# Graph-network kernel: a table lookup by one-hot matmuls on four quarter tiles of the array instead of two halves

## What is computed

```python
for l in range(3):
    f1 = relu(x[row] @ nb_W[l] + nb_b[l])
    f2 = relu(x[col] @ self_W[l] + self_b[l])
    h = relu(concatenate([f1, f2], axis=1) @ att1_W[l] + att1_b[l])
    log_alpha = (h @ att2_W[l] + att2_b[l])[:, 0]
    mask = clip(sigmoid(log_alpha) * (ZETA - GAMMA) + GAMMA, 0.0, 1.0)
    rowsum = segment_sum(mask, row, num_segments=n) + 1e-06
    d_inv_sqrt = clip(rowsum ** (-0.5), 0.0, 10.0)
    vals = mask * d_inv_sqrt[row] * d_inv_sqrt[col]
    x = segment_sum(vals[:, None] * x[col], row, num_segments=n)
    out = out + x
```

## Time and profile before

| what | us |
|---|---|
| median of 3 runs (11231.23 to 11239.19) | 11238.58 |
| span of the profiled execution, first to last instruction | 10215.4 |
| median less span (what lies around the span) | 1023.2 |
| TensorE busy in the span (matmuls) | 8439.0 |
| VectorE busy | 8039.4 |
| GpSimd busy | 4364.3 |
| ScalarE busy | 3166.6 |

### The profile page before, as it was taken

How to read it: one execution, slowest core, us unless ns; L and a number is a source line. 1 busy time by engine, 2 the same in 40 slices (tenths; PEclk the granted TensorE clock), 3 DMA queues, 4 the chain that set the end, 5 groups by cost and what they waited for, 6 DMA issues and landing times. The chain is left out here.

```text
span 10215.4 us, 720231 instructions
## 1 busy us (share of the span) xinstructions
PE 8439.0 (83%) x288671; PEld 7571.9 (74%) x288671; DVE 8039.4 (79%) x13908; ACT 3166.6 (31%) x6110; POOL 4364.3 (43%) x4880
## 2 busy tenths in 40 slices
PE   0113288888887999899997999899997999879996
PEld 0112177877776888799997888799997888768885
DVE  9998488888887777777777777777777777777775
ACT  0110156666663333300002333300001333333332
POOL 0002601111116888311114888521112888758883
PEclk9755599999998999999998999999998999989996
DMA  1001277777765555577775555467775555545552
GB/s 27 0 0 27 49 226 232 230 230 232 229 216 143 162 161 160 142 212 214 211 212 155 161 159 161 130 205 212 212 214 170 161 161 160 141 130 160 159 161 70
DMA packets 1005301, 1633.48 MB, mean 160 GB/s; under 512 B 260439, under 2 KB 743635, under 8 KB 1004831
## 3 DMA queue, kind: packets, MB, share of 16 engines
q1 hardware_dynamic: 954104, 1581.29, 52.8%
q0 software_dynamic: 51104, 50.97, 2.3%
HBM read 1345.54 MB, written 286.24 MB: 160 GB/s over the span
## 5 line engine op out<-in xcount | busy, mean ns | idle before, releaser
L1034 PE MATMUL bank<-tab,extra 128*64 128x64 bf16 x201684 | 3981.3, 197 | 389.0 <-DMA extra<-one_hots 230.4
L1034 PEld LDWEIGHTS bank<-tab,extra 128*64 128x64 fp8e4 x201684 | 3566.3, 112 | 877.4 <-issue 817.2
L739 POOL TENSOR_TENSOR planes<-planes 128x448 f32<-128x448 f32 (+1 forms) x2744 | 2610.2, 963 | 542.5 <-DVE planes L1767 476.1
L888 ACT CAST bank<-planes 128x448 f32<-128x448 bf16 (+1 forms) x2744 | 1515.1, 552 | 2289.5 <-DVE planes L1760 2283.0
L1142 PE MATMUL bank<-planes,extra 128*128 128x192 bf16 x19992 | 2098.2, 247 | 43.1 <-POOL planes L739 10.0
L669 POOL DMA_INDIRECT xg<-q_table,ixb x588 | 561.1, 954 | 3592.0 <-ACT ixb L837 3486.3
L1760 DVE TENSOR_TENSOR planes<-bank,mask_all 128x448 f32<-128x448 f32 (+2 forms) x2744 | 1699.0, 619 | 274.2 <-PE bank L1034 171.0
L1767 DVE TENSOR_TENSOR planes<-planes,bank 128x448 f32<-128x448 f32 (+1 forms) x2744 | 1727.4, 630 | 126.5 <-ACT bank L888 126.4
L1142 PEld LDWEIGHTS bank<-planes,extra 128*128 128x128 fp8e4 x19992 | 1584.2, 96 | 172.7 <-issue 55.0
L1640 DVE SCALAR_TENSOR_TENSOR extra<-bank,a2w 128x448 f32<-128x448 f32 (+1 forms) x2058 | 1300.2, 640 | 510.2 <-PE bank L1059 453.7
L1059 PE MATMUL bank<-plb,extra 128*128 128x64 bf16 x44982 | 1595.9, 194 | 14.4 <-ACT plb L869 9.0
(11 more groups left out here) (227 smaller groups left out, 4734.3 us busy)
## 6 DMA issues: line engine op xcount, KB each, us to landing
extra<-one_hots SPq DMA_DIRECT2D x1372, 368.0 KB, 3.3
extra<-one_hots SPq DMA_DIRECT2D x2156, 224.0 KB, 3.6
extra<-one_hots SPq DMA_DIRECT2D x588, 192.0 KB, 2.4
one_hots<-extra SPq DMA_DIRECT2D x490, 224.0 KB, 2.3
one_hots<-extra SPq DMA_DIRECT2D x294, 368.0 KB, 3.9
work<-slot_rows_cols SPq DMA_DIRECT2D x196, 368.0 KB, 5.2
work<-slot_rows_cols SPq DMA_DIRECT2D x294, 224.0 KB, 4.0
work<-slot_rows_cols SPq DMA_DIRECT2D x98, 192.0 KB
```

The lines of the kernel that those rows point to most:

```text
L739: nc.gpsimd.tensor_tensor(tiles(yrl[:, 2, a * C:b * C]), tiles(yrl[:, 1, a * C:b * C]), upper[:, 1, a:b, :], ALU.subtract).then_inc(low_re ...
L888: nc.scalar.copy(tiles(z_banks[g][:, 0:(b - a) * C]), upper[:, 0, a:b, :]).then_inc(high_ps, 1)
L1034: mm = pe.matmul(bank[half * S:(half + 1) * S, i * C:(i + 1) * C], oct_[:, k * P + half * S:k * P + (half + 1) * S], tab[:, at:at + C], st ...
```

## The change

In `cols`, a half tile of 64 slots is done as two quarters of 32 slots. The four quarters of a tile use four column quarters of the array and partitions 0, 32, 64 and 96 of the bank. The loops are turned round: the plane is outside, the quarters inside. Every matmul still moves 64 columns; there are 12 per tile instead of 6, each with a weight load of 32 columns instead of 64. Nothing else in the program differs.

```diff
+Q = 32
...
-                    for half in range(2):
-                        b = 2 * k + half
-                        for pl in range(NPL):
-                            at = (pl * NB + b) * C
-                            mm = pe.matmul(bank[half * S:(half + 1) * S, i * C:(i + 1) * C],
-                                           oct_[:, k * P + half * S:k * P + (half + 1) * S], tab[:, at:at + C],
+                    for pl in range(NPL):
+                        for q in range(4):
+                            at = (pl * NB + 2 * k + q // 2) * C
+                            mm = pe.matmul(bank[q * Q:(q + 1) * Q, i * C:(i + 1) * C],
+                                           oct_[:, k * P + q * Q:k * P + (q + 1) * Q], tab[:, at:at + C],
                                            start=(i == 0 and pl == 0), stop=True, skip_group_check=True)
```

## The result

The changed kernel takes 13,086.1 us (median of 4 runs, 13,084.0 to 13,095.0) beside 11,235.7 us for the kernel before on the same chip: ratio 1.165, 95% interval 1.163 to 1.167. It is slower by 16%; the forecast was 11,064 us and the range ended at 12,150. The profiled execution has a span of 13,083.9 us, 1.7 us less than its time as the runs are timed. So the 1,023 us that stood "around the span" ahead of the prediction did not exist; what they were, the experiments show.

What follows compares the result with a forecast made beforehand. TensorE was taken to bound six of seven loops. Lookups -225, first layer's edges -10 and code +60 gave -175 us, so 11,238.6 became 11,064 us; the range ran from 10,990 to 12,150.

Steps and rivals of the forecast that it cites:

- 1,023 us: Difference between the earlier kernel's profiled span and its median time, added unchanged to the predicted span of 10,040 us.
- Part (4): TensorE's code: more instructions mean more packets fetched in loops' first turns; nothing to 73 us, counted as +60.
- part (1): Lookups: a round falls from 31.9 to 29.3 ns as narrower weight loads hide; -225 us in six loops.
- rival D: Loops no longer fit where code is kept and are fetched each turn: +3,700 us, chance 0.04.
- What has to hold: Condition on the sequencer: hand over 24 instructions per tile in 88 ns, one per 3.7 ns.
- rival A: The sequencer becomes the bound in lookups; at 5.0 ns per instruction 12,000 us, chance 0.24.
- Part (3): VectorE, ScalarE, GpSimd and SyncE's loads keep their instructions and each wait stays in place; no cost counted.
- Rival B: Four streams in the array hinder each other, 36.9 ns per round: 11,730 us, chance 0.10.
- Part (2): Switches between full and split array, between lookups and scatters: number unchanged, cost put at nothing.
- TensorE bounds six loops: TensorE limits six of seven loops over the 98 blocks; small gains pass in full, losses at once.
- what would show it: Signs to look for in the profile: the long lookup run's length, block times, some 85 packets and none inside a loop.

Runs made afterwards that it cites:

- e5: The changed kernel run again, nothing else altered: 11,958.1 us beside 10,219.7 for the kernel before.
- e6: The changed kernel with 205 satisfied waits added at the start of TensorE's program: 11,134.3 us, 91 packets.
- f1: The changed kernel moved by 205 waits, with GpSimd's two indirect DMAs per block replaced by a clearing of the rows: 10,850.1 us; kernel before 11,252.7.
- f2: The kernel before, with GpSimd's two indirect DMAs per block replaced by a clearing of the rows: 10,323.3 us beside 11,252.7.
- e12: The same kernel as e6, timed in rounds on another chip: 12,361.3 us, ratio 1.090 to the kernel before.
- e8: The changed kernel with quarters only in every other tile of 128 slots, halves in the rest: 13,813.2 us.
- e2: The changed kernel with halves kept in the first layer's edges, quarters everywhere else: 12,760.2 us, 858 packets.
- e11: The changed kernel with 115 satisfied waits at the start of TensorE's program in place of 205: 15,991.4 us, 1,817 packets.
- f4: The kernel before, unchanged, profiled on a slower chip: 11,252.7 us.
- g2: The kernel before, with the second gather of each edge block waiting for group 1: 10,799.9 us beside 11,332.7, ratio 0.953.

## Why the prediction failed, step by step

The sum of -225 - 10 + 60 us failed at all its large terms. Part (4) counted code at 60 us, and one loop that is fetched again costs 824. Waits between groups and GpSimd's gathers stood at nothing; once TensorE uses instructions as fast as they come, they make most of the other 900. And part (1)'s -225 did not come.

On chips X the loss of 1,738 us (e5) splits into 824 us of code fetched again (e5 less e6), 527 us that stay without gathers (f1 less f2, on a chip Y), and the rest, 387 us, by the gathers. The 527 are carried over from one kind of chip to the other, so the last two are estimates. On chips Y e12 has 1,010 us without refetching, of which some 480 by the gathers. There the kernel before is torn in its edges, too, and the change adds almost nothing to later edges.

- **Part (4), code at +60 us, and rival D at 0.04.** The largest miss: 824 us for one loop fetched again on every second turn. Rival D named the mechanism, and its question was right ("no row here shows a loop of more than 4.5 packets"), but it was put aside by a figure for the whole memory. The loop of 6.8 packets is refetched or not by where its first instruction falls in a packet. D was right in kind for one of seven loops and wrong in size: it had every turn of all seven fetched, +3,700 us, at 3.0 us a packet. One turn of this loop takes 35 to 36 us and the next 19 to 22, with nine packets for the two, about 4 us apart.
- **What has to hold, and rival A.** The supply gives one instruction per 4.15 ns, slower than the 3.7 needed and quicker than the 5.0 at which the rival was priced. So this rival had the mechanism. By itself that is 24 x 4.15 = 100 ns per tile against 95.4: 0.2 us per block. What the rival missed is that the supply now has nothing in hand. The kernel before used an instruction per 7.95 ns, and 64 lay ready, 0.5 us of work. This stock covered every wait between groups, which costs 181 to 211 ns from start to start inside a run of f1 and does not show in f2, and on chips X it covered the gathers. With the 0.2 us the waits make 0.9 us per block of segment sums and 0.5 per block of later edges, some 450 us (f1 less f2); the first layer's edges lose nothing, and the rest of the 527 lies in the first turns of the loops and between them, where part (4) had put its 60.
- **Part (3), "GpSimd keeps its instructions", at nothing.** It keeps them, and their side effect, 387 us on chips X, had been covered by that stock. That the stock is what covered it is argued from its size (0.5 us) and the gaps' (0.23 to 0.34 us on chips X, up to 0.75 on chips Y, where halves are torn, too); no run changed the stock alone. No sum over TensorE's own rows could show it; the runs on chips Y did.
- **The 1,023 us between span and median.** They were taken as lying around the span. They were mostly the gathers' gaps on another chip: on one such chip 929 of 1,033 us go with them (f2). A gap of 10% between a profile and the runs that nothing explains was the one sign, ahead of the prediction, that TensorE could be starved.
- **Part (1), rounds of 29.3 ns.** Right while instructions lie ready: 29 ns for the rounds of four after the first, in the first 8 rounds of a run. The saving is gone by the end of the run: 84 quarters last as long as 42 halves. So the term of -225 us was worth nothing. Rival B, four streams in each other's way, is false: starts 3 to 4 ns apart and no longer round. This is what the Trainium skill's figure of some 4 ns per further tile (TensorE: Matmul & The Clock Gate, the section on packing small matmuls) says; the trace agrees.
- **Part (2), switches at nothing.** Their number did not change, and nothing shows a cost. A switch between the two widths is worth 125 ns (e8).
- **TensorE bounds six loops, a loss passes through at once.** Right.
- **Slips that change little.** The first edges' block has 843 matmuls, which makes 13.8 packets and +5 us, not 12.9 and +3. The second packet of the earlier trace rows lies 0.55 us into its window, not 0.8; the 6543.1 is right. Rival A at 5.3 ns with the code's 60 us would be 12,206; 12,150 belongs to about 5.2 ns.

Of what would show it: the run of 276 lasts 2.76 us (2.38 the 138 before), over rival A's mark of 2.7, and the packets rose to hundreds.

```profile
6005.44 2.76 PE L1034 MATMUL bank<-tab,extra 128*32 128x64 bf16 x276 [0.21 <-issue]
6008.40 0.86 PE L1059 MATMUL bank<-plb,extra 128*128 128x64 bf16 x24 [0.20 <-issue]
```

## What to carry to other kernels

Count instructions per microsecond, and not only busy time: an engine that uses them as fast as they come has no stock left, and every wait, hold-up or fetch that was hidden before is paid in full. A loop of TensorE that comes near 1,600 instructions should be kept shorter or looked at in its place in the program (the one of 1,616 was fetched again in e2 and e11, the one of 1,318 never); 205 idle instructions ahead of it were worth 7% here. If the same program is 10% slower in timed runs than in its profile, find out what the timed runs wait for before costing a change.

## What the runs showed of the hardware that was not expected

- A loop of 1,746 instructions of TensorE costs 9 us per turn more when it lies over eight packets of 16 KB, by count, than over seven (e5, e6), and 17 us more in a third place (38.0 us per turn in e11, 20.9 in e12, one chip); 90 instructions' difference at the start of the program made 3,630 us (e11, e12).
- TensorE's instructions stop for 0.2 to 0.75 us beside an indirect DMA on which GpSimd works for 0.96 us, and longest on chips Y (f1 to f4). In the profile such a gap is "issue"; it does not name GpSimd, and only the two timelines side by side show it.
- The kernel before takes 10,216 to 10,221 us on three chips and 11,236 to 11,351 on others; on one of these, 929 of 1,033 us go when the gathers are left out. On such a chip, setting two gathers 4 us apart in place of 1.25 brings 4.7% (g2).
- TensorE takes instructions at about 4.15 ns each when none lie ready. About 64 lay ready at the start of a run (32 matmuls and their loads start in 0.23 us).
- Lookups of two widths are dear to mix: 123 to 126 ns per switch, 4.6 us per block of segment sums with 42 of them (e8).
